# Routing in smaller batches, norms with the sign turned, a shared layer by channels, and weight copies ahead of row copies

## The chip, the cores and the metric

The kernel runs on one core of a Trainium2 chip. Its engines are TensorE (PE, with its weight loads listed as PEld), VectorE (DVE), ScalarE (ACT), GpSimd (POOL) and SyncE (SP), which here only issues DMAs. Each engine works through its own list of instructions in order, and semaphores tie the lists together. The metric is device time in microseconds of one launch, lower is better; times are medians of several runs.

## The reference, cut to what matters

The input `x` is 16 x 256 tokens of 128 channels, so 4096 tokens. One block of a recurrent mixer (RWKV) is followed by a layer norm and a mixture of experts with a shared expert:

```python
x = _layernorm(x + _L0_attn_ref(x, ...))     # three norms inside, k/v/r, a scan over time, channel mixing
# _L0_ffn_ref
ys = _geglu(xf @ Ws1 + bs1) @ Ws2 + bs2      # shared expert, 256 hidden channels
logits = (xf @ Wr + br) / TAU                # 12 experts, the two best per token
top_val, top_idx = jax.lax.top_k(logits, 2)
top_w = jax.nn.softmax(top_val, axis=-1)
act = _geglu(einsum('nd,edh->enh', xf, We1) + be1)   # 384 hidden channels for each expert
yE = einsum('enh,ehd->end', act, We2) + be2
x = _layernorm(x + ys + einsum('end,ne->nd', yE, w))
```

All in float32. The kernel computes an expert only for the tokens that chose it.

## The kernel before

**First stages.** The 4096 tokens are cut into 8 chunks of 512 (`CH`, `CT = 4` tiles of 128 each). Every chunk passes norm 0, norm 1, keys, values and receptance, the scan, the output projection, norm 2, the channel mixing, norm 3, the turn into channels (`xnT_all`), the router and the shared expert. These steps are small functions (`stats1(c)`, `turn2(c)`, `hidden(c, j)` and so on), and each engine has a list of calls, written out by hand, that sets its order: chunks overlap like the stages of a pipeline. A norm is `stats` on DVE, `deviation(c, n)` on POOL (`over_deviation`, L811 to L819: add epsilon, negate the mean, raise to the power -1/2, multiply) and `apply` on ACT.

**Routing.** `chosen(v, b)` picks the two best experts of a batch of chunks on DVE, `prefix(b)` counts on PE, `placed(v, b)` turns the counts into places, and `scatter_rows` on POOL sends the rows with 64 indirect DMAs (two per tile of tokens) into `dispatched_rows`, a region for each expert. `BATCH` gives the chunks of a batch: four batches of two chunks. When the last batch is placed, `find_tiles` on DVE writes `pad_at` and signals `rows_known`; SP then sends 12 blocks of padding, and `tell_tiles` writes `word`, the list of tiles with their experts, and signals `tiles_known`.

**Shared expert.** `shared_gate`, `shared_up`, `shared_gelu`, `shared_act`; `shared_back` multiplies by `Ws2` with tokens as output rows (eight 128-wide matmuls and four with the bias), `shared_take` on ACT copies the result into `xnT_all`, and POOL adds it to `x_all` (L1129, eight adds of 128x512 at the head of the expert stage, `sh_added`).

**Loop over tiles.** There are 75 tiles (`TILES`) of 128 dispatched rows. SP copies the rows of tile n into `xg[n % 10]` (`load_rows`, L1093, 68 KB) and the expert's first weights into `w1[n % 5]` (`load_weights`, L1100, 384 KB). PE does, for tile n: `gate_of` and `up_of` (three products each, L1244), `turn_x(n + 2)` (L1236), `second(n - 1)` (L1262, and the bias L1231). ACT does `gelu_of`; DVE does `act_of(n)` (L1165) and `give_y(n - 1)` (L1172); POOL sends each result to `routed_rows`. Once in five tiles DVE also does `where_to` (L1150 to L1157), which computes for the next five tiles where their rows go, and for that waits until all five have been copied:

```python
for n in range(r * U, (r + 1) * U):
    v.wait_ge(x_loaded2[n % XB], (n // XB + 1) * 16)
```

It stands in DVE's list after `act_of(n)` and `give_y(n - 1)` for n = 2, 7, 12, ..., 67 (`if n % U == 2 and n + U < TILES: where_to(n // U + 1)`), so 14 times in the loop, and `where_to(k + 1)`, at n = 5k + 2, needs rows 5k + 5 to 5k + 9. Two waits of the loop matter beside it: `up_of(n)` waits for `act_of(n - 1)`, whose bank it overwrites, and `load_weights(n)` waits for `up_ready` of tile n - 5, whose weight buffer it overwrites. SP's list reads rows five tiles ahead of weights: after five row copies, `load_weights(n)`, `load_rows(n + 5)` for each n.

**End.** SP waits for all results, loads the two results of each token (`y_first` into `x0_all`, `y_second` into `xnT_all`), PE adds three terms in PSUM for each chunk (`add_to`, L1290), and the last norm follows on DVE, POOL and ACT.

## Time and profile before

| what | value |
| --- | --- |
| median of 3 runs | 470.45 us (469.33 to 470.94) |
| profiled execution, its own time | 469.14 us |
| span of its trace | 467.4 us |
| busy PE / DVE / ACT / POOL | 405.8 / 313.4 / 273.0 / 271.0 us |
| mean granted PE clock | 0.961 of full |

The trace has three parts: the first stages with routing up to about 252 us, the loop over tiles from 261.67 us to about 436 us, and the end. In the trace L1093 is a copy of rows, L1100 a copy of weights, L1150 the first instruction of a `where_to`. The span starts with the first instruction, and the 1.7 us between span and time lie around it. A time that a row gives for PE ends where the model of the pipelined matmul puts it.

### The profile page before, as it was taken

How to read it: one execution, taken by the hardware profiler on the slowest of the kernel's cores; microseconds unless marked ns; L12 is line 12 of the kernel's file. 1: busy time of each engine (PE TensorE's matmuls, PEld its weight loads, DVE VectorE, ACT ScalarE, POOL GpSimd, SP SyncE). 2: the span in 40 equal slices, each digit the busy share in tenths (PEclk: the TensorE clock that was granted, in tenths of full speed). 3: DMA queues.
4: the chain of work that ended last, by engine and by line, in shares of the span. 5: the costliest groups of instructions: out<-in, count | busy, mean ns of one | idle time of the engine just before them, and what ended most of it. 6: DMA issues, size and time to landing. Idle time of an engine off the chain costs nothing.

```text
span 467.4 us, 9975 instructions
## 1 busy us (share of the span) xinstructions
PE 405.8 (87%) x2658; PEld 321.1 (69%) x2658; DVE 313.4 (67%) x1057; ACT 273.0 (58%) x648; POOL 271.0 (58%) x360
## 2 busy tenths in 40 slices
PE   0176799998989897999998698999999999999991
PEld 0133466765655583877666698999999999999530
DVE  4669889999999999644831555555655555655162
ACT  2476599998978766595532354455545555554055
POOL 4766757586567867788777543444444444444264
PEclk9997789999999898999999599999999999999997
DMA  5389900000001000111132566666666666764393
GB/s 153 90 169 356 280 1 0 1 1 2 0 2 42 24 31 14 44 37 48 61 108 67 181 225 222 233 232 241 243 233 239 228 230 231 249 234 174 120 325 113
DMA packets 49261, 64.09 MB, mean 137 GB/s; under 512 B 9916, under 2 KB 32188, under 8 KB 49208
## 3 DMA queue, kind: packets, MB, share of 16 engines
q1 hardware_dynamic: 44760, 54.08, 34.8%
q0 software_dynamic: 4448, 9.38, 6.0%
q8 instruction: 24, 0.39, 0.4%
q14 instruction: 29, 0.24, 0.2%
HBM read 20.87 MB, written 13.91 MB: 74 GB/s over the span
## 4 chain that ended last, share of the span: by engine, by line
PE 54%; DVE 12%; POOL 12%; issue 9%; DMA 5%; ACT 4%; SPq 2%; ACTq 0%; DVEq 0%; POOLq 0%
PE bank L1244 23%; PE bank L1262 11%; POOL dispatched_rows L407 7%; PE bank L956 4%; PE bank L974 4%; PE bank L907 2%; PE bank L908 2%; DVE bst L478 2%; PE bank L1236 2%; PE bank L985 1%; DMA xnT_all<-routed_rows 1%; PE bank L986 1%; POOL rstd L817 1%; POOL frs L817 1%; ACT z L683 1%
## 5 line engine op out<-in xcount | busy, mean ns | idle before, releaser
L1133 POOL DMA_INDIRECT routed_rows<-yo,goes_to x75 | 71.8, 958 | 102.3 <-DVE yo L1172 99.6
L1244 PE MATMUL bank<-xT,w 128*128 128x128 f32 x900 | 119.6, 284 | 5.8 <-DMA w<-we_sb 3.9
L1244 PEld LDWEIGHTS bank<-xT,w 128*128 128x128 f32 x900 | 108.9, 195 | 8.3 <-issue 5.8
L1208 ACT ACTIVATE gl<-bank,tile_bias 128x128 f32<-128x128 f32 x225 | 66.7, 365 | 60.3 <-PE bank L1244 59.3
L1165 DVE SCALAR_TENSOR_TENSOR actT<-bank,tile_bias,gl 128x128 f32<-128x128 f32 x225 | 65.7, 345 | 31.4 <-PE bank L1244 25.4
L407 POOL DMA_INDIRECT dispatched_rows<-rows_all,slot_i x64 | 64.2, 1003 | 18.5 <-issue 17.3
L1262 PE MATMUL bank<-we_sb,actT 128*128 x450 | 62.7, 276 | 1.0 <-DVE yo L1172 0.9
L1262 PEld LDWEIGHTS bank<-we_sb,actT 128*128 128x128 f32 x450 | 56.1, 192 | 1.4 <-issue 1.4
L1172 DVE TENSOR_SCALAR yo<-bank,goes 128x128 f32<-128x128 f32 x75 | 26.3, 350 | 33.6 <-PE bank L1231 33.4
L956 PE MATMUL bank<-xk,wfk_sb 128*128 128x512 f32 x64 | 34.2, 649 | 5.2 <-DVE xk L575 4.2
L1202 ACT ACTIVATE xT<-bank 128x128 f32<-128x128 f32 x75 | 20.8, 277 | 28.9 <-PE bank L1236 28.2
L817 POOL TENSOR_TENSOR rstd<-veps,half 128x4 f32<-128x4 f32 x32 | 35.0, 1093 | 2.5
L907 PE MATMUL bank<-hT,mixa 128*128 128x512 f32 x48 | 28.4, 677 | 4.4 <-ACT hT L711 4.1
L974 PEld LDWEIGHTS bank<-wfv_sb,kf 128*128 128x128 f32 x256 | 29.5, 192 | 2.8 <-ACT kf L768 2.2
L893 PE MATMUL bank<-ident,z 128*128 128x128 f32 x64 | 10.7, 294 | 23.5 <-ACT z L683 23.5
L974 PE MATMUL bank<-wfv_sb,kf 128*128 128x128 f32 x256 | 30.2, 276 | 0.5 <-ACT kf L768 0.5
L814 POOL TENSOR_TENSOR veps<-mv,eps 128x4 f32<-128x4 f32 x32 | 8.7, 272 | 34.2 <-DVE mv L483 31.1
L893 PEld LDWEIGHTS bank<-ident,z 128*128 128x128 f32 x64 | 8.0, 151 | 28.5 <-issue 22.8
L558 DVE RECIPROCAL rec<-nd 128x512 f32<-128x512 f32 x8 | 26.7, 3341 | 0.7 <-POOL nd L861 0.7
L908 PE MATMUL bank<-hT,mixb 128*128 128x512 f32 x48 | 26.6, 638 | 0.0
L612 DVE SCALAR_TENSOR_TENSOR below_m<-bank,v_sb,below_p 128x512 f32<-128x512 f32 x16 | 11.9, 747 | 18.8 <-PE bank L1009 10.4
L956 PEld LDWEIGHTS bank<-xk,wfk_sb 128*128 128x128 f32 x64 | 11.6, 201 | 15.8 <-issue 7.0
(204 smaller groups left out, 824.2 us busy)
## 6 DMA issues: line engine op xcount, KB each, us to landing
w<-we_sb SPq DMA_DIRECT2D x75, 384.0 KB, 2.7
x_all<-dispatched_rows SPq DMA_DIRECT2D x75, 68.0 KB, 2.0
we_sb<-we SPq DMA_DIRECT2D x1, 4608.0 KB
rows_all<-x SPq DMA_DIRECT2D x8, 256.0 KB, 2.7
x_all<-routed_rows SPq DMA_DIRECT2D x8, 256.0 KB, 4.8
xnT_all<-routed_rows SPq DMA_DIRECT2D x8, 256.0 KB, 6.6
out<-x_all SPq DMA_DIRECT2D x8, 256.0 KB, 2.3
routed_rows<-yo,goes_to POOLq DMA_INDIRECT x75
```

What stands on the lines that cost most here:

```text
L407: ng.indirect_dma_start(dispatch, bass.IndirectOffsetOnAxis(ap=slot_i[:, k, n:n + 1], axis=0), rows_all[:, n, :], None).then_inc(s["dispat ...
L558: nv.reciprocal(rec[:, :], nd[:, 1, :]).then_inc(s["rec_ready"], 1)
L817: ng.tensor_tensor(rs[:, :], ve[:, :], half[:, :], ALU.pow).then_inc(step, 1)
L907: nt.matmul(o, mixa[:, n, :], hT[:, :, 1:T + 1], start=True, stop=False)
L908: nt.matmul(o, mixb[:, n, :], hT[:, :, 0:T], start=False, stop=True).then_inc(s[name], 1)
L956: nt.matmul(pf[j % 2][:, :], wfk_sb[:, j * P:(j + 1) * P], xk2[:, :], start=True, stop=True).then_inc(s["fk_ready"], 1)
L974: last = nt.matmul(pkv[:, n * P:(n + 1) * P], kf[:, j, n * P:(n + 1) * P], wfv_sb[:, j, :], start=j == 0, stop=j == HF - 1)
L1133: ng.indirect_dma_start(routed, bass.IndirectOffsetOnAxis(ap=goes_to[n // U % DB][:, n % U:n % U + 1], axis=0), yo[n % YO][:, :], None).th ...
L1165: nv.scalar_tensor_tensor(actT[n % UA][:, at], ps_a[j][:, 0:P], tile_bias[:, j, n:n + 1], gl[n % 2][:, at], ALU.add, ALU.mult).then_inc(s2 ...
L1208: na.activation(gl[n % 2][:, j * P:(j + 1) * P], ps_g[j][:, 0:P], ACT.Gelu, bias=tile_bias[:, HK + j, n:n + 1]).then_inc(s2["gelu_ready"], 1)
L1244: return nt.matmul(to[:, 0:P], w1[m][:, off:off + P], xT[m][:, :], start=True, stop=True)
L1262: nt.matmul(ps_y[:, 0:C], actT[m][:, j * P:(j + 1) * P], we2_sb[:, ds(e, 1), j, :].rearrange("p a c -> p (a c)"), start=j == 0, stop=False)
```

## The change

1. `BATCH` has six batches: chunk 0, chunks 1 and 2, chunks 3 and 4, then 5, 6 and 7 alone. The lists of DVE, ACT, POOL and PE for the first stages are written in another order, with the 64 scatters spread otherwise over POOL's list: 26 stand behind the last `deviation(7, "3")`, 28 before.
2. In norms 0, 1 and 2 the mean is no longer negated. `mv` has a third column of -1, one POOL instruction multiplies mean and -1 by the deviation, and ACT so applies the norm with its sign turned; the weights `ln0w`, `LN1W`, `LN2W` are negated once in `prepare` (`turned_sign`).
3. `shared_back` gives channels as output rows with two 128x512 matmuls, and `shared_take` on DVE adds the bias and the chunk of `xnT_all` in place. The eight adds on POOL are gone. In the end `add_turned` (four 128-wide matmuls a chunk) takes `xnT_all` back to tokens, and `y_second` lands in `x_all`, whose rows are 136 numbers apart.
4. SP issues the five weight copies of tiles 0 to 4 as soon as `tiles_known` is there, ahead of the wait for the scatters. Behind them stand the five row copies, and then, for n = 5 and up, `load_rows(n)` and `load_weights(n)`.

```diff
-    BATCH = ((0, 2), (2, 4), (4, 6), (6, 8))
+    BATCH = ((0, 1), (1, 3), (3, 5), (5, 6), (6, 7), (7, 8))
...
-        y_second = xnT_all[:, :].rearrange("p (n c) -> p n c", c=C)
+        y_second = x_all
...
+            def shared_take(c):
+                if c == 0:
+                    v.wait_ge(s["bias_loaded"], 2 * 16)
+                v.wait_ge(s2["sh_out"], c + 1)
+                at = slice(c * W, (c + 1) * W)
+                nv.scalar_tensor_tensor(xnT_all[:, at], sh_y[:, :], bs2_col, xnT_all[:, at], ALU.add, ALU.add).then_inc(s2["sh_taken"], 1)
...
-            shared_act(2, 0); shared_act(2, 1); logits(7); chosen(v, 3); shared_act(3, 0); shared_act(3, 1)
-            placed(v, 3, pT[:, PT_PREFIX]); find_tiles(); shared_act(4, 0); shared_act(4, 1); tell_tiles()
+            shared_act(3, 1); shared_take(2); placed(v, 5, pT[:, PT_PREFIX]); shared_act(4, 0); shared_act(4, 1)
+            shared_take(3); find_tiles(); shared_act(5, 0); shared_act(5, 1); shared_take(4); tell_tiles()
...
-                over_deviation(g, veps[n], negm[n], rstd[n], nmr[n], mv[n], s["pow" + n], c, s["nmr" + n])
+                if n == "3":
+                    over_deviation(g, veps[n], negm3, rstd[n], nmr3, mv[n], s["pow" + n], c, s["nmr" + n])
+                else:
+                    ng.tensor_tensor(veps[n][:, :], mv[n][:, :, 1], eps4[:, :], ALU.add).then_inc(s["pow" + n], 1)
+                    g.wait_ge(s["pow" + n], c * 2 + 1)
+                    ng.tensor_tensor(rstd[n][:, :], veps[n][:, :], half[:, :], ALU.pow).then_inc(s["pow" + n], 1)
+                    g.wait_ge(s["pow" + n], c * 2 + 2)
+                    ng.tensor_tensor(both[n][:, :, :], mv[n][:, :, 0:3:2], over(rstd[n][:, :], 2), ALU.mult).then_inc(s["nmr" + n], 1)
...
-                for n in range(CT):
-                    for j in range(HS):
-                        nt.matmul(sh_y[:, n * P:(n + 1) * P], ash[:, j, n * P:(n + 1) * P], ws2_sb[:, j, :],
-                                  start=j == 0, stop=False)
-                    last = biased(sh_y[:, n * P:(n + 1) * P], BS2, C)
+                for j in range(HS):
+                    last = nt.matmul(sh_y[:, :], ws2_sb[:, j, :], ash[:, j, :], start=j == 0, stop=j == HS - 1)
...
-            sp.wait_ge(s2["tiles_known"], 1)
-            sp.wait_ge(s["dispatched"], SLOTS // P * 16)
-            sp.wait_ge(s2["pads_placed"], E * 16)
...
+            sp.wait_ge(s2["tiles_known"], 1)
+            for n in range(U):
+                load_weights(n)
+            sp.wait_ge(s["dispatched"], SLOTS // P * 16)
+            sp.wait_ge(s2["pads_placed"], E * 16)
             for n in range(U):
                 load_rows(n)
-            for n in range(TILES):
+            for n in range(U, TILES):
+                load_rows(n)
                 load_weights(n)
-                if n + U < TILES:
-                    load_rows(n + U)
...
-            g.wait_ge(s["dispatched"], SLOTS // P * 16)
-            for c in range(CH):
-                at = slice(c * CT, (c + 1) * CT)
-                g.wait_ge(s2["sh_taken"], c + 1)
-                ng.tensor_tensor(x_all[:, at, :], x_all[:, at, :], shared_out[:, at, :], ALU.add).then_inc(s2["sh_added"], 1)
...
+            def add_turned(c):
+                for n in range(CT):
+                    at = slice(n * P, (n + 1) * P)
+                    nt.matmul(banks[c][:, at], xnT_all[:, c * W + n * P:c * W + (n + 1) * P], ident[:, :], start=n == 0, stop=False)
```

**SP's list where the expert stage begins.** `w1_0` to `w1_4` are the weight buffers; `x0_all` stands for the row buffers `xg`, which lie in it. The last block of padding and what follows it, before:

```order
L1082 DMA dispatched_rows<-pad_rows 16x1088
L1088 TENSOR_LOAD word [waits e_pads_placed,dispatched,e_tiles_known]
L1093 ISA
L1093 DMA x0_all<-dispatched_rows 128x136
L1088 TENSOR_LOAD word
```

The same place now, and further down where the row copies begin:

```order
L1098 DMA dispatched_rows<-pad_rows 16x1088
L1108 TENSOR_LOAD word [waits e_tiles_known]
L1112 REGISTER_ALU
L1112 ISA
L1112 DMA w1_0<-we1_sb 128x768
```

```order
L1112 DMA w1_4<-we1_sb 128x768
L1100 TENSOR_LOAD word [waits e_pads_placed,dispatched]
L1105 ISA
L1105 DMA x0_all<-dispatched_rows 128x136
L1100 TENSOR_LOAD word
```

The first weight copy stood behind five row copies; now all five weight copies stand between the padding and the first row copy, and the wait for the scatters comes after them.

**SP's list at rows 9.** Before, from the weight copy of tile 4 to that of tile 5 (the row copy between them is that of tile 9):

```order
L1100 DMA w1_4<-we1_sb 128x768
L1088 TENSOR_LOAD word
L1093 ISA
L1093 DMA x0_all<-dispatched_rows 128x136
L1096 TENSOR_LOAD word
L1100 REGISTER_ALU [waits e_up_ready]
L1100 ISA
L1100 DMA w1_0<-we1_sb 128x768
```

Now, from the row copy of tile 8 on; the weight copy is that of tile 8 and the row copy behind it that of tile 9:

```order
L1100 TENSOR_LOAD word
L1105 ISA
L1105 DMA x0_all<-dispatched_rows 128x136
L1108 TENSOR_LOAD word
L1112 REGISTER_ALU [waits e_up_ready]
L1112 ISA
L1112 DMA w1_3<-we1_sb 128x768
L1100 TENSOR_LOAD word
L1105 ISA
L1105 DMA x0_all<-dispatched_rows 128x136
L1108 TENSOR_LOAD word
```

Row copy 9 stood ahead of the first weight copy that waits for `up_ready`; now it stands behind four of them, the last of which waits for tile 3. The same holds for every later tile: row copy n stood behind the wait for tile n - 10, and stands behind the wait for tile n - 6.

**DVE's list where the last batch is placed.** The first row is the last instruction of the last `placed`, `pad_at` opens `find_tiles`. Before:

```order
L377 CAST slot_i<-slot 128x2x8 [waits route]
L617 CAST pad_at<-run 1x12
L619 TENSOR_SCALAR run_i<-run 128x12 [waits e_tiles_step]
L620 MEMSET wait_here 1x1 [waits e_tiles_step]
L621 TENSOR_SCALAR run_t<-run_i 128x12
```

Now:

```order
L378 CAST slot_i<-slot 128x2x4 [waits route]
L619 SCALAR_TENSOR_TENSOR below_m<-bank0,v_sb,below_p 128x512 [waits e_sh_out,e_sh_gelu,e_sh_up]
L619 SCALAR_TENSOR_TENSOR below_m<-bank2,v_sb,below_p 128x512 [waits e_sh_gelu,e_sh_up]
L627 SCALAR_TENSOR_TENSOR xnT_all<-bank7,braw,xnT_all 128x512 [waits e_sh_out]
L631 CAST pad_at<-run 1x12
L633 TENSOR_SCALAR run_i<-run 128x12 [waits e_tiles_step]
L634 MEMSET wait_here 1x1 [waits e_tiles_step]
```

Three instructions of the shared expert of chunks 4 and 3 have moved ahead of `find_tiles`, and with it of `rows_known`, for which SP waits.

## Rows read from the trace of the kernel before

**Rows 1.** The page: the chain that ended last, by line.

```profile
PE bank L1244 23%; PE bank L1262 11%; POOL dispatched_rows L407 7%; PE bank L956 4%; PE bank L974 4%; PE bank L907 2%; PE bank L908 2%; DVE bst L478 2%; PE bank L1236 2%; PE bank L985 1%; DMA xnT_all<-routed_rows 1%; PE bank L986 1%; POOL r
```

**Rows 2.** Timeline, the loop: start us, us, engine, line, operation, [idle before <-releaser].

```profile
314.30 0.51 SPq L1100 DMA_DIRECT2D w<-we_sb  x1
...
314.55 1.56 PE L1244 MATMUL bank<-xT,w 128*128 128x128 f32 x12
...
315.42 0.34 SPq L1093 DMA_DIRECT2D x_all<-dispatched_rows  x1
...
316.77 1.56 PE L1244 MATMUL bank<-xT,w 128*128 128x128 f32 x12
...
317.36 0.17 DVE L1150 TENSOR_TENSOR other<-x_all,own_code 128x5 f32<-128x5 f32 x1
```

**Rows 3.** Timeline, DVE alone, near the end of the loop.

```profile
419.60 0.17 DVE L1150 TENSOR_TENSOR other<-x_all,own_code 128x5 f32<-128x5 f32 x1 [0.48 <-DMA x_all<-dispatched_rows]
```

**Rows 4.** Timeline, the one place where the loop waited for rows.

```profile
283.45 0.89 PE L1244 MATMUL bank<-xT,w 128*128 128x128 f32 x6
...
284.62 0.17 DVE L1150 TENSOR_TENSOR other<-x_all,own_code 128x5 f32<-128x5 f32 x1 [2.78 <-DMA x_all<-dispatched_rows]
...
285.35 0.87 DVE L1165 SCALAR_TENSOR_TENSOR actT<-bank,tile_bias,gl 128x128 f32<-128x128 f32 x3
...
285.75 1.01 PE L1244 MATMUL bank<-xT,w 128*128 128x128 f32 x6 [1.42 <-DVE actT L1165]
...
287.79 1.58 PE L1244 MATMUL bank<-xT,w 128*128 128x128 f32 x12
```

**Rows 5.** One line (L1100): duration ns min/median/max, first to last start.

```profile
L1100 SPq FUSED_REGOPS  x75: 46/52/57, 258.6 to 423.2; - x75
L1100 SPq DMA_DIRECT2D w<-we_sb x75: 486/492/595, 258.7 to 423.3; - x75
```

**Rows 6.** Timeline, PE alone: the two restarts after a wait.

```profile
34.17 1.64 PE L907 MATMUL bank<-hT,mixa 128*128 128x512 f32 x2 [3.26 <-ACT hT L711]
...
180.65 2.20 PE L956 MATMUL bank<-xk,wfk_sb 128*128 128x512 f32 x3 [2.25 <-DVE xk L575]
```

**Rows 7.** Stretches: us, busy of PE, PEld, DVE, ACT, POOL; PEclk, DMA, GB/s.

```profile
34.83:38.24 3.41, 3.41 (x9) 1.59 (x8) 3.38 (x7) 2.36 (x7) 2.37 (x3) 0.53 0.79 225
80.00:100.00 20.00, 19.86 (x108) 13.45 (x107) 19.76 (x55) 17.59 (x36) 13.91 (x21) 1.00 0.01 1
181.60:185.02 3.42, 3.42 (x5) 1.24 (x4) 3.35 (x7) 1.65 (x4) 2.77 (x4) 0.53 0.00 0
284.00:287.41 3.41, 1.94 (x14) 1.52 (x14) 2.52 (x11) 1.08 (x4) 0.66 (x1) 1.00 0.59 206
...
46.00:48.00 2.00, 2.00 (x10) 2.00 (x11) 1.92 (x17) 1.53 (x3) 1.54 (x3) 0.50 1.02 401
50.00:52.00 2.00, 2.00 (x4) 0.74 (x3) 1.73 (x10) 1.73 (x5) 0.40 (x1) 0.57 1.06 293
```

**Rows 8.** Timeline, from the last scatters to the first tiles.

```profile
229.69 0.15 DVE L617 CAST pad_at<-run 1x12 int32<-1x12 f32 x1
...
231.26 15.06 SPq L1082 DMA_DIRECT2D dispatched_rows<-pad_rows  x12
...
254.02 1.56 PE L1043 MATMUL bank<-of_expert,be_sb 12*128 12x75 f32 x12
254.42 3.78 SPq L1093 DMA_DIRECT2D x_all<-dispatched_rows  x5
...
259.81 0.27 DVE L1150 TENSOR_TENSOR other<-x_all,own_code 128x5 f32<-128x5 f32 x1 [8.21 <-DMA x_all<-dispatched_rows]
...
260.12 1.19 DVE L1152 TENSOR_TENSOR moved<-x_all,other 128x10 f32<-128x10 f32 x1
...
261.67 2.90 PE L1244 MATMUL bank<-xT,w 128*128 128x128 f32 x12 [3.90 <-DMA w<-we_sb]
```

**Rows 9.** One line (L407), the scatters: duration ns, first to last start.

```profile
L407 POOL DMA_INDIRECT dispatched_rows<-rows_all,slot_i x64: 954/958/1433, 142.0 to 251.6; - x64
```

More of the change, by code:

```diff
@@ new lines, in attention_vector @@
+            weigh_v(5); output(4); stats1(7); states(5); stats2(4); maximum(6); logits(2); gaps(6); carried(5)
+            x3(3); stats3(3); mix(4); one_over(5); output(5); chosen(v, 1); weigh_v(6); stats2(5); states(6)
+            carried(6); placed(v, 1, pT[:, PT_PREFIX]); maximum(7); gaps(7); mix(5); x3(4); logits(3)
+            one_over(6); output(6); stats3(4); weigh_v(7); stats2(6); states(7); carried(7); x3(5); stats3(5)
+            mix(6); one_over(7); logits(4); output(7); chosen(v, 2); shared_act(0, 0); stats2(7)
@@ L987, in rwkv @@
                 last.then_inc(s["po_ready"], 1)
-            def biased(to, row, width):
-                return nt.matmul(to, ones_bf[:, :], bias_rows[:, ds(row, width)], start=False, stop=True)
             def bank_read(c, j, of, first, other):
@@ L1296, in experts_tensor @@
             for c in range(CH - 1):
-                add_to(c, x_all, first=True)
+                add_turned(c)
             t.wait_ge(s2["yo_ready"], TILES)
-            add_to(CH - 1, x_all, first=True)
+            add_turned(CH - 1)
             for c in range(CH):
```

211 lines of the change are left out of this document (107 added, 104 removed).

## The prediction

> **What bounds the kernel now.** I read the chain of waits first, by line [rows 1]. Its largest shares are L1244 and L1262, the matmuls of the loop over tiles, then the scatters L407. So two places count: the loop, bound by PE, and the handover to it, where PE waits. The loop's timeline comes next [rows 2]. Tile 22 begins on PE at 314.55 and tile 23 at 316.77, so a tile takes 2.22 us and PE has no gap. Look there at two other rows: SP issues the rows of tile 29 at 315.42, and the `where_to` that waits for them (L1150) starts at 317.36, hardly before DVE must go on to tile 23. Row copies arrive just in time even now. Third, the one place where they did not [rows 4]: L1150 waited 2.78 us until 284.62, and PE then stood still for 1.42 us. At the handover [rows 8] SP sends padding for 15.06 us from 231.26, row copies from 254.42, and PE's first tile waits for its weights until 261.67. The first stages keep both PE and DVE over 98% busy between 80 and 100 us [rows 7], so a new order alone has little to give there.
>
> **Row copies behind the weights' waits: the large term.** In the new list the rows of tile 5k+9 stand behind the weight copy of tile 5k+8, and that waits for `up` of tile 5k+3. But `where_to(k+1)` stands in DVE's list ahead of `act_of(5k+3)` and needs these rows, and PE's `up(5k+4)` waits for `act_of(5k+3)`. So each of the 14 `where_to` becomes a closed chain, priced step by step:
> - end of `up(5k+3)` to SP's weight copy: 0.1 us from the register step to the DMA [rows 5], with the semaphore and one more step 0.3 (an estimate);
> - weight copy to row copy on SP: 314.30 to 315.42, 1.12 us [rows 2];
> - row copy to the start of L1150, whose data it is: 315.42 to 317.36, 1.94 us [rows 2];
> - L1150 to PE's next matmul: 284.62 to 285.75, 1.13 us [rows 4].
>
> That is 4.49 us. Without a wait, `up` of one tile ends at 316.11 (314.55 + 1.56), and that of the next begins 0.67 us after 316.77 (twelve matmul instructions take 1.56, six take 0.89 [rows 2, 4]), at 317.44: 1.33 us. PE thus gains a hole of 4.49 - 1.33 = 3.16 us. Behind the wait at 285.75 the next tile began 2.04 us later [rows 4] where 1.55 is normal, so add 0.49. Five tiles take 5 x 2.22 + 3.65 = 14.8 us at full clock.
>
> **The clock on top.** PE's restart after 3.26 us idle at 34.17 and after 2.25 us at 180.65 [rows 6] was each followed by a stretch at 0.53 granted clock, from 34.83 and from 181.60 [rows 7], that is nearly all at 1.2 GHz instead of 2.4. Half the speed for 3.4 us costs 1.7 us. After the shorter hole of 1.42 us the clock stayed at 1.00, from 284.00 on [rows 4, 7]. A hole of 3.16 lies with the first two. I take 1.2 us for each of the 14: most of 1.7, less for a slow stretch that begins inside the hole, and for DVE's 0.49, which it covers. Bounds are 0 and 1.7. Five tiles then take 16.0 us (14.8 to 16.5), against 11.25 now (284.62 to 419.60 in twelve steps [rows 3, 4]).
>
> **The handover.** The early weight copies look like a gain: PE waited 3.90 us for weights at 261.67 [rows 8]. But they stand on SP behind the padding, and `find_tiles`, which starts the padding, moves behind two `shared_act` and one `shared_take`. I put `pad_at` at 235 instead of 229.69. Then padding runs from 236.6 to 251.7, five weight copies at about 1.05 us (0.49 issue [rows 5] and the load of `word`) to 256.9, and the first row copy goes out at 257.5, not 254.42. The first `where_to` starts at 262.9 instead of 259.81 (3.1 later), but its steps take some 0.2 us each as in the loop, not 1.19 [rows 8], since the POOL adds that ran beside them are gone. DVE's first `act_of` so starts at 263.6, within 0.2 of now. Nothing is gained. If `find_tiles` came at its old time, 3 us would be, and this end stays in the range. From 263.6, tiles 1 to 3, the first of them at half clock as now, bring `up(3)` to its end at 270.1 and the second `where_to` to 273.5.
>
> **The scatters.** POOL's 64 scatters end at 251.6 [rows 9] and bind SP now. Two fewer behind the last norm would free about 2.5 us (1.26 us each), but SP is not ready for them until 256.9. So batches of other sizes and 26 instead of 28 weigh nothing, unless POOL ends more than 5 us later than now. The two further batches repeat `chosen` and `placed` on DVE, after the stages in which DVE is full. For the new order of the first stages, the shorter norm chain on POOL and the cheaper second layer together I take -1 us, from bounds of -6 and +4. The second layer and `tell_biases` (254.02 now [rows 8]) lie hidden in front of the first tile; if that cover were gone, each microsecond would count once.
>
> **The end.** `y_second` now lands in rows of 512 bytes. Both kinds of transfer stand in the loading of the experts' weights: 401 GB/s with pieces of 3 KB (46 to 48 us) and 293 GB/s with pieces of 512 bytes (50 to 52 us) [rows 7]. For 2.1 MB that is 5.2 against 7.2 us. Part of it hides behind the final norm, so +1 us (0 to 2). The Trainium skill, DMA: Bandwidth & Descriptors, section Specifications, says that pieces from 512 bytes up reach line rate, which would make this term 0; the rows here say otherwise.
>
> **The sum.** The second `where_to` at 273.5, the third at 289.5, the last, twelve steps of 16.0 later, at 481.5, against 419.60: +61.9. Behind the last one PE resumes within its hole and slow stretch, +0.9. With -1 and +1 that is +62.8 on the profiled execution's 469.14, so 532; I take 531. The runs' median is 1.3 us above the profile, which the range covers.
>
> **The rivals.**
> 1. *The clock stays.* The hole comes as above, but no slow stretch: 14 x 1.2 = 17 less, 514 us. For it speaks the hole of 1.42; against it those of 2.25 and 3.26. The Trainium skill, TensorE: Matmul & The Clock Gate, section HAM oscillation — how this bites in real kernels, warns only of idle gaps longer than this hole. By that rule it would be this case; the restart at 180.65 contradicts it, since a hole of 2.25 was enough. Chance 0.27.
> 2. *The handover pays and the loop does not lose.* Place: row copy against DVE, once in five tiles. It decides whether rows are there 0.2 us (1.33 - 1.13) after `up(5k+3)` ends; I get 3.36. For it speaks that SP today meets its weight waits late, with the awaited tile long done, so a wait in its list costs nothing now. Against it, that this holds only while SP lags, and that here the awaited tile is the one before the hole. The wait of rows 4 would go too (-2.1), with -1 and +1: 467 us. Chance 0.04.
> 3. *Row copies land later.* They now go out just behind 384 KB of weights and beside POOL's scatters; one microsecond more on each of the 14 gives 545 or above. Against it: the copy at 315.42 went out behind weights as well. Chance 0.07.
> 4. *The order has no effect,* all is hidden: within 0.3% of now. Chance 0.02.
>
> **How the numbers follow.** My case, holes with a slower clock after most, has 0.60: 531 us, its own range 522 to 540. The range 507 to 545 takes in rival 1 with 7 us below it for a handover and first stages that gain (3 + 5, less 1), and on top 7 us if every hole brings the full 1.7 (14 x 0.5) and 7 for slower copies. Outside are rivals 2 and 4 and most of 3. A measurement of this kernel can tell about 0.3% from no change. Slower by more: 0.95; faster: 0.04, rival 2; same: 0.01.
>
> **What would show it.** In the trace of the changed kernel L1150's counterpart should wait for `x_all<-dispatched_rows` some 3 to 5 us, 14 times, with PE idle 3 us each time behind DVE's `actT`; the distance of two `where_to` should be 16 us; SP's weight copy should start 0.3 us after `up` ends; the granted clock in the loop should fall from 1.00 to about 0.9, where rival 1 has it at 1.00. The first row copy should go out near 257.5, right behind five weight copies. I am wrong if distances stay at 11.25, which would mean that SP runs further ahead than its list allows; or, in size, if landing or clock differ from the rows used.

## The result, and where the time went

The changed kernel takes 551.0 us (median; 550.6 to 554.2) against 470.1 us before: 1.172 of the time, 95% interval 1.167 to 1.178. In a later group, which also held the kernel before, it took 546.2 us (1.159, 1.155 to 1.163). The forecast was 531, its range ended at 545. Direction and mechanism are those of the forecast, the size is not. The profiled execution of the changed kernel took 554.23 us, its span is 552.5.

The chain of waits, by line, has turned over [rows 1]. SP's queue and DMA, which had 2% and 5% of it, now hold a quarter:

```profile
PE 37%; DVE 23%; SPq 18%; issue 9%; DMA 8%; POOL 4%; ACT 1%; DVEq 0%; ACTq 0%; POOLq 0%
PE bank L1253 14%; DMA x_all<-dispatched_rows 6%; SPq L1112 5%; PE bank L1271 5%; SPq L1108 3%; SPq L1105 3%; PE bank L981 3%; SPq L1100 3%; PE bank L999 2%; DVE rec L565 2%; DVE bst L485 2%; PE bank L932 2%; PE bank L933 2%; SPq L1098 1%;
```

Who waits for whom in the loop (284 to 520 us), in total, times, longest. VectorE's L1159 is the first instruction of `where_to`; before, eight of these 14 waited for rows, 5.7 us in sum and 2.78 at most [rows 3, 4]:

```profile
DVE other L1159 <- DMA x_all<-dispatched_rows: 65.4, 14, 5.6
...
PE bank L1253 <- DVE actT L1174: 46.7, 14, 4.3
```

One of the 14 closed chains, on the timeline of the changed kernel (start, duration, engine, line):

```profile
396.28 1.56 PE L1253 MATMUL bank<-xT,w 128*128 128x128 f32 x12
...
398.25 0.49 SPq L1112 DMA_DIRECT2D w<-we_sb  x1
...
398.51 0.89 PE L1253 MATMUL bank<-xT,w 128*128 128x128 f32 x6
...
399.33 0.34 SPq L1105 DMA_DIRECT2D x_all<-dispatched_rows  x1
401.26 0.17 DVE L1159 TENSOR_TENSOR other<-x_all,own_code 128x5 f32<-128x5 f32 x1 [4.32 <-DMA x_all<-dispatched_rows]
...
402.38 1.00 PE L1253 MATMUL bank<-xT,w 128*128 128x128 f32 x6 [2.99 <-DVE actT L1174]
...
403.55 1.64 PE L1271 MATMUL bank<-we_sb,actT 128*128 x6
...
405.09 2.36 PE L1253 MATMUL bank<-xT,w 128*128 128x128 f32 x12
```

Read it from the top: `up` of tile 5k+3 ends at 397.84 (396.28 + 1.56), SP's weight copy starts 0.41 later, the row copy 1.08 behind it, `where_to` 1.93 behind that, and PE resumes 1.12 later: 4.54 us where the forecast had 4.49. PE does `gate` of the next tile in between and stands still for 2.99 us. Soon behind it, the six instructions of L1271 take 1.64 us (0.83 at 397.78, ahead of the pause), and the tile after it 2.36 us for twelve instead of 1.56. The clock of the same place (stretch, busy time of PE, PEld, DVE, ACT, POOL; granted clock, DMA share, GB/s):

```profile
400.00:402.00 2.00, 0.00 (x0) 0.00 (x0) 0.64 (x5) 0.00 (x0) 0.00 (x0) 1.00 0.34 113
402.00:404.00 2.00, 1.58 (x9) 1.33 (x10) 1.88 (x8) 0.28 (x1) 0.62 (x1) 0.84 0.00 0
404.00:406.00 2.00, 2.00 (x11) 1.94 (x11) 0.35 (x1) 0.13 (x1) 0.34 (x1) 0.50 0.66 226
```

So the slow stretch, at 1.2 instead of 2.4 GHz, begins here some 1 us after PE is back at work. Whole distances between two `where_to`, same columns:

```profile
302.11:319.77 17.66, 13.34 (x100) 12.81 (x100) 6.52 (x24) 6.03 (x20) 4.79 (x5) 0.90 0.44 151
...
386.41:401.26 14.85, 11.80 (x100) 11.25 (x100) 6.53 (x25) 5.81 (x20) 4.79 (x5) 1.00 0.52 180
401.26:417.50 16.24, 13.28 (x100) 12.73 (x100) 6.52 (x24) 6.03 (x20) 4.79 (x5) 0.89 0.47 164
...
433.79:450.94 17.15, 14.25 (x100) 13.95 (x100) 6.99 (x25) 6.03 (x20) 4.79 (x5) 0.80 0.45 156
```

The second row is the chain alone at full clock: 14.85, forecast 14.8. The third holds the slow stretch above, which ends at 406.8, and takes 16.24. The fourth takes 17.15: its slow stretch is twice as long and unbroken. It began in the pause, ahead of PE's return at 434.92, and went on to about 440.9 (same columns):

```profile
433.50:434.50 1.00, 0.00 (x0) 0.00 (x0) 0.60 (x4) 0.00 (x0) 0.00 (x0) 0.79 0.02 8
...
439.50:440.50 1.00, 1.00 (x7) 1.00 (x6) 0.41 (x2) 0.40 (x2) 0.39 (x1) 0.50 0.12 39
440.50:441.50 1.00, 1.00 (x9) 1.00 (x9) 0.65 (x2) 0.28 (x1) 0.00 (x0) 0.80 0.18 61
```

The first row has the shorter stretch and a row copy that landed late.

The handover, on the timeline [rows 8]:

```profile
244.04 0.15 DVE L631 CAST pad_at<-run 1x12 int32<-1x12 f32 x1
...
245.60 15.07 SPq L1098 DMA_DIRECT2D dispatched_rows<-pad_rows  x12
...
261.23 5.19 SPq L1112 DMA_DIRECT2D w<-we_sb  x5
...
267.09 4.92 SPq L1105 DMA_DIRECT2D x_all<-dispatched_rows  x6
...
270.99 2.85 PE L1253 MATMUL bank<-xT,w 128*128 128x128 f32 x12 [0.28 <-issue]
```

Padding and weight copies lie 0.56 us apart, weight and row copies 0.67, so SP has no idle time there, as forecast, but `pad_at` comes at 244.04 instead of 235.

### The profile page after: what moved, and what is told of

Same layout as the page of the kernel before. It is cut to its first block, busy times and chain, and to the rows that moved or that the text cites. A ratio compares the mean times of both kernels' runs of the same rounds, so it can differ in the third digit from the quotient of the medians.

```text
span 552.5 us, 9846 instructions
## 1 busy us (share of the span) xinstructions
PE 436.3 (79%) x2580; PEld 342.6 (62%) x2580; DVE 332.9 (60%) x1119; ACT 277.3 (50%) x646; POOL 256.5 (46%) x328
## 3 DMA queue, kind: packets, MB, share of 16 engines
q1 hardware_dynamic: 47400, 54.08, 29.5%
## 4 chain that ended last, share of the span: by engine, by line
PE 37%; DVE 23%; SPq 18%; issue 9%; DMA 8%; POOL 4%; ACT 1%; DVEq 0%; ACTq 0%; POOLq 0%
PE bank L1253 14%; DMA x_all<-dispatched_rows 6%; SPq L1112 5%; PE bank L1271 5%; SPq L1108 3%; SPq L1105 3%; PE bank L981 3%; SPq L1100 3%; PE bank L999 2%; DVE rec L565 2%; DVE bst L485 2%; PE bank L932 2%; PE bank L933 2%; SPq L1098 1%; POOL frs L833 1%
## 5 line engine op out<-in xcount | busy, mean ns | idle before, releaser
L1253 PE MATMUL bank<-xT,w 128*128 128x128 f32 x900 | 140.7, 311 | 47.0 <-DVE actT L1174 46.7
L1253 PEld LDWEIGHTS bank<-xT,w 128*128 128x128 f32 x900 | 126.8, 219 | 51.5 <-DVE actT L1174 49.4
L1217 ACT ACTIVATE gl<-bank,tile_bias 128x128 f32<-128x128 f32 x225 | 69.2, 366 | 69.3 <-PE bank L1253 67.7
L1174 DVE SCALAR_TENSOR_TENSOR actT<-bank,tile_bias,gl 128x128 f32<-128x128 f32 x225 | 67.7, 346 | 35.7 <-PE bank L1253 31.0
L1271 PE MATMUL bank<-we_sb,actT 128*128 x450 | 70.9, 299 | 1.3 <-DVE yo L1181 0.9
L1271 PEld LDWEIGHTS bank<-we_sb,actT 128*128 128x128 f32 x450 | 63.6, 213 | 3.3 <-issue 3.2
L1159 DVE TENSOR_TENSOR other<-x_all,own_code 128x5 f32<-128x5 f32 x15 | 2.5, 166 | 76.3 <-DMA x_all<-dispatched_rows 76.3
L999 PEld LDWEIGHTS bank<-wfv_sb,kf 128*128 128x128 f32 x256 | 29.4, 192 | 2.3 <-ACT kf L789 1.9
L861 POOL TENSOR_TENSOR rstd<-veps,half 128x4 f32<-128x4 f32 x24 | 27.2, 1132 | 1.9
L1245 PE MATMUL bank<-ident,x_all 128*128 128x128 f32 x75 | 22.6, 302 | 6.8 <-DMA x_all<-dispatched_rows 6.8
L785 ACT ACTIVATE kf<-bank 128x512 f32<-128x512 f32 x32 | 18.8, 591 | 12.3 <-PE bank L981 12.2
```

The costliest lines, as they stand in the source:

```text
L999: last = nt.matmul(pkv[:, n * P:(n + 1) * P], kf[:, j, n * P:(n + 1) * P], wfv_sb[:, j, :], start=j == 0, stop=j == HF - 1)
L1174: nv.scalar_tensor_tensor(actT[n % UA][:, at], ps_a[j][:, 0:P], tile_bias[:, j, n:n + 1], gl[n % 2][:, at], ALU.add, ALU.mult).then_inc(s2 ...
L1217: na.activation(gl[n % 2][:, j * P:(j + 1) * P], ps_g[j][:, 0:P], ACT.Gelu, bias=tile_bias[:, HK + j, n:n + 1]).then_inc(s2["gelu_ready"], 1)
L1253: return nt.matmul(to[:, 0:P], w1[m][:, off:off + P], xT[m][:, :], start=True, stop=True)
L1271: nt.matmul(ps_y[:, 0:C], actT[m][:, j * P:(j + 1) * P], we2_sb[:, ds(e, 1), j, :].rearrange("p a c -> p (a c)"), start=j == 0, stop=False)
```

## The experiments

Sixteen kernels (two of them twice) ran in five groups, each beside the kernel before, and ratios are to that. Every group had another chip. In three groups the kernel before took 470 to 471 us, in the first and the fourth 497 and 495. On those two chips VectorE and ScalarE stand still for up to 17 us at a time, mostly between 200 and 275 us (the waits of those traces name "remote"; the other traces have none). SP's padding is longer there too: 29.2 to 29.7 us in the kernels with the old order of the first stages and 16.5 to 20.4 in those with the new one, where the other chips show 15.1 to 15.6. So the ratios of these two groups say little about the handover. Distances in the loop are as elsewhere (16.58 us there with closed chains, 16.54 and 16.77 on other chips).

**1. The loop: which part of the change makes the chain.** Rows five tiles ahead again in the changed kernel, early weights kept:

```diff
-            for n in range(U, TILES):
-                load_rows(n)
-                load_weights(n)
+            for n in range(TILES):
+                if n >= U:
+                    load_weights(n)
+                if n + U < TILES:
+                    load_rows(n + U)
```

> The changed kernel with one edit on SP: the five weight copies stay early, but behind the first five row copies the list is again row copy n+5 behind weight copy n, so that rows run five tiles ahead. My theory (all of the loop's loss is the closed chain row copy - weight wait - where_to): the distance of two where_to falls from 16.8 to 11.25 us, the granted clock in the loop is 1.00 again, and what is left against the kernel before is the later handover (second where_to at 284 against 273) and 0 to 1 us at the end: 480 to 483 us. Rival (the early weights, the shared layer or the changed buffers slow the loop as well): distances stay above 12 us and the time above 490 us.

Measured: 1.0069 (1.0036 to 1.0102). The whole time is less than expected (480 to 483 us would be 1.020 to 1.027). The likely reason, which no run shows, is that on this chip the old order loses in the padding, 29.4 us against 16.5, what the later `pad_at` costs the new one. For the loop my theory held: the mean distance of two `where_to` is 11.37 us, at full clock, and PE is busy for 147.11 of 147.84 us:

```profile
304.31:452.15 147.84, 147.11 (x1308) 144.83 (x1307) 86.80 (x313) 75.81 (x263) 62.24 (x65) 1.00 0.66 232
```

The new SP list of part 4, put alone into the kernel before:

> The kernel before with part 4 of the change alone (five weight copies ahead of the wait for the scatters, then rows and weights of the same tile in turn). My theory: distances of 16 to 17 us as in the changed kernel, 13 times 5.5 us or 72 us, the first hole on top and 1 to 2 us less at the handover: 540 to 546 us. Rival (the clock is pulled down by more than the holes, the first stages have a part in it): distances of 14.8 us at full clock and 515 us.

Measured: 1.1498 (1.1462 to 1.1535), 74 us, mean distance 16.58 us, as expected (540 to 546 us would be 1.148 to 1.160). The full-clock distance appears here too, beside one with a clock of 0.80:

```profile
407.68:424.63 16.95, 14.01 (x100) 13.71 (x100) 6.92 (x24) 6.03 (x20) 4.80 (x5) 0.80 0.45 158
424.63:439.74 15.11, 11.81 (x100) 11.25 (x100) 6.53 (x24) 5.81 (x20) 4.80 (x5) 1.00 0.50 176
```

So the row copies' place in SP's list is needed and is enough for what the loop loses; the first stages have no part in that. Third, SP's list stays as changed and VectorE's list moves:

```diff
-                if n % U == 2 and n + U < TILES:
+                if n % U == 4 and n + U < TILES:
```

> The changed kernel with SP's list as it is, and where_to two tiles later in VectorE's list (n = 4, 9, 14 ... instead of 2, 7, 12 ...). The rows of tile 5k+9 still go out only behind up(5k+3), but where_to no longer stands ahead of the act that PE needs next. My theory: copies land 3.4 us behind up(5k+3) and where_to comes up about 3.3 us behind it, so it waits 0 to 0.5 us, PE has no holes, distances are 11.25 us: 480 to 484 us, the same as with rows ahead. Rival (late row copies hurt by themselves, through turn_x or because SP then waits for where_to in turn): 490 us or more.

Measured: 1.0206 (1.0163 to 1.0249), 506 us on this slower chip; as a ratio that is my theory (480 to 484 us would be 1.020 to 1.029). Mean distance 11.77 us. This is one of the fourteen:

```profile
318.61 0.58 SPq L1105 DMA_DIRECT2D x_all<-dispatched_rows  x1
...
318.85 0.17 DVE L1159 TENSOR_TENSOR other<-x_all,own_code 128x5 f32<-128x5 f32 x1 [1.23 <-DMA x_all<-dispatched_rows]
...
319.22 1.77 PE L1253 MATMUL bank<-xT,w 128*128 128x128 f32 x12
```

VectorE still waits 1 to 1.5 us in eight of them (2.92 once), but PE's next step mostly does not stand behind it. It did once: behind the wait of 2.92 us PE paused for 1.63 us until 425.85, and the granted clock of that distance is 0.86. Two tiles of distance in one list give back 13 times 4.8 us against `b_new_list` on the same chip. Nothing was done to SP or the copies, so late row copies cost little by themselves.

**2. The clock.** Ten products that nobody uses, put into the hole:

```diff
                 gate_of(w, n, r)
+                if w == U - 1 and n + 1 < TILES:
+                    t.wait_ge(s2["xT_ready"], n + 2)
+                    for _ in range(10):
+                        nt.matmul(ps_x[:, P:2 * P], ident[:, :], ident[:, :], start=True, stop=True)
                 up_of(w, n)
```

> The changed kernel with ten 128x128 products of the identity that nobody uses, into free columns of ps_x, between gate and up of the last tile of every five (n = 4, 9, ... 69), so right in the hole that PE has there: ten products take about 2.7 us, the hole is 2.9 to 4.4. It does more work and computes the same. My theory (part of the loss is the slower clock after the hole, 1.4 us for one slow stretch, 2.3 us for two): PE is never idle, the granted clock stays near 1.00, and the distance of two where_to falls from 16.5 to about 14.9 us: 521 to 527 us, a ratio of 1.11 against 1.159. Rival (the slow stretches come from something else than PE's pause, the products only add to the chain): 546 us or more, a ratio of 1.16.

Measured: 1.1478 (1.1448 to 1.1507), 540.4 us: faster, but less gained than I expected (1.11). The 1.159 is from another group and chip, and this kernel's trace has the slow stretch of point 5, which the trace behind 1.159 has not. The traces show the loop by itself: from the second to the last `where_to` it takes 205.0 us, against 218.0 and 215.1 in the changed kernel's two. The trace has one hole filled like this (L1292 are the extra products), and the clock of the distance that ends in it:

```profile
409.63 2.40 PE L1292 MATMUL bank<-ident 128*128 128x128 f32 x20
412.60 0.17 DVE L1159 TENSOR_TENSOR other<-x_all,own_code 128x5 f32<-128x5 f32 x1 [5.26 <-DMA x_all<-dispatched_rows]
```

```profile
396.82:412.60 15.78, 14.04 (x120) 13.49 (x120) 6.52 (x24) 5.81 (x20) 4.78 (x5) 1.00 0.49 169
```

Eleven of the 13 distances now show a clock of 1.00; in the changed kernel it was one of 13 (two of 13 in its second trace). More work made the kernel faster, so the slow stretches do come from PE's pauses. The mean distance fell from 16.77 and 16.54 to 15.77, not to 14.9: VectorE's waits for rows grew (the 13 after the second `where_to` sum to 65.2 us, 60.2 in the changed kernel), so part of the gain went to later row copies. Why they land later there, no run tells.

**3. The early weight copies.** In the kernel before, alone:

> The kernel before with the five weight copies early and the row copies still five tiles ahead. My theory: PE's first tile no longer waits 3.9 us for weights but begins when its row copy has landed, near 258 us; VectorE's first act then hangs on where_to(0), so only part of it is gained: 468 to 469 us, 1 to 2 us less than before. Rival A (all 3.9 us are gained): 466 us. Rival B (weight copies beside the scatters delay the scatters, and with them the rows): 470 us or more.

Measured: 0.9989 (0.9965 to 1.0012): smaller than the interval. This is one of the slower chips: the padding lasts 29.35 us, to 278.2, and the weight copies follow at 278.80, so SP had next to no idle time to use, and the run does not test early copies where it has. In the changed kernel, taken back (all of SP's list as before, so that parts 1 to 3 are left):

> The changed kernel with all of SP's list as before (rows five tiles ahead, no early weight copies). My theory: in the changed kernel SP is never idle between find_tiles and the first rows (15.1 us of padding to 260.7, then 5.2 us of weights), so the early copies delay the rows by 5.2 us and save at most 3.9 us at the first tile; taking them back gains 1 to 3 us against the same kernel with them: a ratio of about 1.002 to 1.005 if that kernel has 1.007. Rival (early weights help, as they do in the kernel before by 0.75 us): 1 to 2 us slower than with them.

Measured: 1.0097 (1.0067 to 1.0127), 475.7 us, in one group with the changed kernel at 546.2. Its ratio does not compare with 1.0069, which is from a slower chip, so my 1 to 3 us were not tested by the time. The first tile can be compared. Without early copies:

```profile
265.67 2.90 PE L1252 MATMUL bank<-xT,w 128*128 128x128 f32 x12 [3.83 <-DMA w<-we_sb]
```

and with them, in the changed kernel's second trace, whose `pad_at` is 0.3 us earlier:

```profile
266.01 2.90 PE L1253 MATMUL bank<-xT,w 128*128 128x128 f32 x12 [0.29 <-issue]
```

The wait for weights is gone, and the rows come later by as much: from `pad_at` to the first tile it takes 26.25 us without early copies and 26.89 with them. "Nothing is gained" held.

**4. The first stages.** Here the forecast was furthest off. The yardstick of this group, the changed kernel again:

> The changed kernel as it is, beside the other runs of this group, as their yardstick: 1.172 of the kernel before, unless the chip counts for something; on the chip of the first group, by the kernel before with the new SP list alone (1.150), 1.15 to 1.18.

Measured: 1.159, 546.2 us. Part 3 (shared layer) alone, then part 2 (norms) alone:

> The kernel before with part 3 of the change alone (second layer of the shared expert by channels, shared_take on VectorE, no adds on POOL, y_second into x_all, add_turned at the end). My theory: about even. VectorE has three shared_take of 0.75 us ahead of find_tiles, 1.5 to 2 us later, the first where_to takes 1 us less without POOL's adds beside it, the load at the end costs 1 us: 0 to +2 us. Rival A (the end gains, since the eight POOL adds and the wait for them go): -2 us. Rival B (VectorE is the bound and shared_take counts in full, with the extra slow-down of what runs beside it): +4 us or more.

> The kernel before with part 2 of the change alone (mean no longer negated in norms 0 to 2, weights negated once). POOL saves 24 short instructions, VectorE gains three in prepare and ACT's first affine waits for them. My theory: POOL is not the bound, so -1 to 0 us; 469.5 to 471 us. Rival A (the norm chain is on VectorE's way, each norm 0.2 us shorter): -3 us. Rival B (the three negations, 1 to 2 us at the start where VectorE prepares weights, push everything back): +1 to +2 us.

Measured: 0.9996 (0.9974 to 1.0019) and 0.9943 (0.9922 to 0.9964). The norms gain 1.8 us by the medians and 2.7 by the ratio, more than my -1 to 0 and near rival A's -3; in the trace the last `x3` of the first stages starts at 211.65 instead of 212.62. Both parts together:

> The kernel before with parts 2 and 3 of the change (norms, shared second layer) and nothing else: order, four batches and SP's list as before. It splits the 4.6 us that parts 1 to 3 together cost. My theory: the two add up (0.9943 and 0.9996), 467 to 469 us, so that the new order with six batches alone costs 6 to 8 us. Rival (norms or shared layer only hurt together with each other, by what runs at the same time on POOL and VectorE): 471 us or more, and the order costs 4 us or less.

Measured: 0.9898 (0.987 to 0.9927), on the fourth group's slower chip. So they went side by side with parts 1 to 3 on a chip of 471 us:

> Parts 2 and 3 of the change alone once more, now side by side with parts 1 to 3 on one chip, since the two stood on different chips (0.9898 where the kernel before took 495 us, 1.0097 where it took 471 us). My theory: parts 2 and 3 gain 0.6 to 1.0% on any chip: a ratio of 0.990 to 0.994. Rival (their gain was that chip's, with its long pauses around the handover): 0.997 or more.

> Parts 1 to 3 with SP's list as before, on the same chip as parts 2 and 3 alone. My theory: part 1 (the written order with six batches, find_tiles behind three more instructions) costs 7 to 9 us: a ratio 0.015 to 0.02 above that of parts 2 and 3. Rival (half of the difference was the chips'): 0.010 or less above it.

Measured: 0.9952 (0.9931 to 0.9974), 468.0 us, and 1.013 (1.0078 to 1.0182), 478.4 us. Part 1, the written order with six batches, costs 10.4 us, the other two give back 3. The six times of the second kernel lie between 472.75 and 480.25, and its trace has the slow stretch of point 5; with the time of the earlier group (475.7), whose trace has not, part 1 would cost 7.7.

Are the batches the cause?

```diff
-    BATCH = ((0, 1), (1, 3), (3, 5), (5, 6), (6, 7), (7, 8))
+    BATCH = ((0, 1), (1, 3), (3, 5), (5, 7), (7, 8))
```

> The changed kernel with five batches instead of six: chunks 5 and 6 are routed together, where chunk 6 was; all other calls stand where they stood. My theory (VectorE is the bound of the first stages and a batch costs some 25 small instructions of 0.17 to 0.2 us, two table loads of 1.28 us on ACT lie in its way too): the last placed comes 2 to 3 us earlier, and with it padding, weights and rows: 543 to 544 us, ratio 1.153 to 1.156 against 1.159. Rival (a batch costs nothing, other work fills the time; the larger last batches come later): no change or 1 us slower.

Measured: 1.168 (1.1657 to 1.1702), above both theories, though 1.159 is from another chip. My theory fell: the last `slot_i` starts at 236.10, in the changed kernel's second trace at 236.12, with two table loads of 1.28 us on ACT fewer on the way. The edit also took one `chosen` out from ahead of the last `x3`, and that `x3` starts at 217.58 instead of 217.70; in the gap VectorE waits 2.77 us for ScalarE's `hT` at 203.40, which it did not in the changed kernel. So one batch less moved neither point. The loss of the order is older than the last two batches. Up to the last `x3` (before, and changed kernel, second trace) VectorE, the fourth column, is busy for 11.1 us more, and that `x3` comes 5.1 us later:

```profile
0.00:212.60 212.60, 170.07 (x873) 114.64 (x873) 178.90 (x548) 155.52 (x287) 146.02 (x211) 0.95 0.23 69
```

```profile
0.00:217.70 217.70, 167.80 (x857) 112.10 (x857) 190.00 (x569) 157.09 (x289) 144.23 (x190) 0.96 0.23 69
```

By the instructions' own durations, which sum to 11.9 us more, 4.6 are routing (a fourth `chosen` and smaller batches), 3.4 the scan and its neighbours, which take longer each, and the rest `prepare`, the shared expert and `x3`. That VectorE is the bound there is not shown by it: in both kernels the step ahead of the last `x3` waits for PE, 5.15 us before and 2.88 now. Which calls of the new order cost the 5.1 us no run separates.

And `find_tiles` comes 3.0 us behind the last `slot_i`; before, it was 0.1 us:

```profile
236.12 0.17 DVE L378 CAST slot_i<-slot 128x8 uint32<-128x8 f32 x1
239.12 0.15 DVE L631 CAST pad_at<-run 1x12 int32<-1x12 f32 x1
```

That place was tried in two kernels, one with rows ahead and early weights, one with all of SP's list as before:

```diff
-            shared_act(3, 1); shared_take(2); placed(v, 5, pT[:, PT_PREFIX]); shared_act(4, 0); shared_act(4, 1)
-            shared_take(3); find_tiles(); shared_act(5, 0); ...
+            shared_act(3, 1); shared_take(2); placed(v, 5, pT[:, PT_PREFIX]); find_tiles(); shared_act(4, 0)
+            shared_act(4, 1); shared_take(3); shared_act(5, 0); ...
```

> The changed kernel with rows five tiles ahead and early weights, and find_tiles directly behind the last placed, ahead of two shared_act and one shared_take. My theory: the padding, and with it weights and rows, starts 2.9 us earlier (241.1 instead of 244.0), since SP's list from find_tiles to the first rows has no idle time, so 3 us less than with find_tiles where it stands: ratio about 1.001 if that kernel has 1.007. Rival (the scatters or the shared layer, now 3 us later, end last): less than 1 us gained.

> Parts 1 to 3 of the change with SP's list as before (1.0097), and find_tiles directly behind the last placed. My theory: part of what the order costs is this place: padding 2.9 us earlier, rows 2.9 us earlier as long as the scatters (last at 253.8) do not bind: rows at 255.6 instead of 258.5, 2.5 to 3 us less, ratio 1.003 to 1.005. Rival (the scatters or the shared layer bind instead): less than 1 us less, ratio 1.008 to 1.010.

Measured: 1.0039 (1.0007 to 1.007), where I had expected 1.001, and, on the fourth group's slower chip, 1.0041 (1.001 to 1.0073), as expected. In the first one's trace `pad_at` starts 0.08 us behind the last `slot_i` (241.50 and 241.42), so the padding does start 2.9 us earlier. The first is 1.9 us below `a_old_sp` in the same group, though its profiled execution had the slow stretch described next. No pair that differs in this place alone ran on one chip, so its worth in time, 1.4 and 2.6 us by the ratios across chips, is likely and not shown.

**5. Five microseconds that come and go.** The changed kernel's two traces part at 161 us. In both PE has paused for 3.09 us, in the recorded one and in the second:

```profile
162.07 1.09 PE L918 MATMUL bank<-ident,z 128*128 128x128 f32 x4 [3.09 <-DVE slot_i L378]
```

```profile
161.28 0.63 PE L918 MATMUL bank<-ident,z 128*128 128x128 f32 x4 [3.08 <-DVE slot_i L378]
```

The clock behind it, again first the recorded one:

```profile
163.00:164.00 1.00, 1.00 (x3) 0.48 (x3) 0.89 (x3) 0.80 (x2) 0.70 (x2) 0.50 0.19 65
165.00:166.00 1.00, 1.00 (x2) 0.34 (x1) 1.00 (x2) 1.00 (x2) 1.00 (x1) 0.50 0.21 70
```

```profile
163.00:164.00 1.00, 1.00 (x7) 0.54 (x5) 1.00 (x3) 0.53 (x2) 0.74 (x1) 1.00 0.20 70
165.00:166.00 1.00, 1.00 (x11) 1.00 (x10) 0.96 (x4) 0.97 (x2) 0.69 (x2) 1.00 0.25 73
```

The last `one_over` starts at 190.06 in the one and at 185.13 in the other, and the 4.9 us stay up to `pad_at` (244.04 and 239.12). The pause ends with `placed` of the second batch, which the new order puts into VectorE's full stretch; before, no pause of more than 1.35 us stands there. Ten traces have this order: five with a clock of 1.00 from 162 to 168 us, whose last `one_over` starts at 185.0 to 185.6; four with 0.50, at 190.1 to 190.8; and one with 0.58, at 188.5. So one more pause near 3 us can cost 5 us or nothing. A shorter one can be enough: at this place the kernel before has a pause of 1.35 us until 159.79, and `b_shared` one of 1.34 us until 160.89, and the clock behind them is, in this order:

```profile
161.00:164.00 3.00, 3.00 (x5) 1.02 (x4) 3.00 (x1) 2.80 (x7) 2.66 (x6) 0.50 0.07 23
```

```profile
161.00:164.00 3.00, 3.00 (x8) 1.33 (x9) 2.96 (x10) 2.89 (x5) 2.52 (x6) 1.00 0.14 46
```

**6. A faster kernel.** Parts 2 and 3, early weight copies, rows five tiles ahead, `where_to` one tile later, order and batches as before:

> A try at a better kernel: the kernel before with the norms and the shared second layer of the change, the five weight copies early, rows five tiles ahead, and where_to one tile later in VectorE's list (n = 3, 8, ...), with the order and the four batches of before. My theory: the early weights gain 1 to 2 us, the later where_to takes away the pause of 1.4 us that before has at 285.75, the rest is even: 466 to 469 us, ratio 0.991 to 0.997. Rival (early weights lose to the scatters, as in no gain): 470 to 472 us.

Measured: 0.9837 (0.9812 to 0.9862), 462.6 us, the shortest time of all and better than I expected. Here SP sends the weights while POOL still scatters, and PE starts 4.2 us earlier than before [rows 8]; 2.8 of them are parts 2 and 3 (258.91 in the trace of `b_parts_2_3_again`):

```profile
245.78 5.66 SPq L1110 DMA_DIRECT2D w<-we_sb  x5
...
253.73 8.03 SPq L1103 DMA_DIRECT2D x_all<-dispatched_rows  x10
...
257.50 2.90 PE L1253 MATMUL bank<-xT,w 128*128 128x128 f32 x12 [0.34 <-ACT xT L1211]
```

No `where_to` of its loop waits, the mean distance is 11.23 us. Which of its edits does it:

> The faster kernel (0.9837) with where_to back at n = 2, 7, 12 ...: parts 2 and 3, early weight copies, rows five tiles ahead. My theory: VectorE then waits again for rows now and then, the last where_to comes 1 to 2 us later than in that kernel; 464 to 465 us, ratio 0.986 to 0.989. Rival (where_to one tile later brought nothing, all of the gain is the early copies and the parts): the same 0.984.

> The faster kernel (0.9837) with SP's list as before, so without early weight copies; where_to at n = 3, 8 ... and parts 2 and 3 stay. My theory: PE's first tile waits 3.8 us for its weights again, of which 3 to 4 us are lost (first tile at 260.5 to 261.5 instead of 257.5): 465.5 to 467 us, ratio 0.990 to 0.993. Rival (VectorE's first act, not the weights, was the bound at the first tile): 463.5 us or less, ratio 0.986.

Measured, both on the fourth group's slower chip: 0.9819 (0.9767 to 0.9872) with `where_to` back, 0.9878 (0.9837 to 0.9918) without early copies, and 0.9898 for parts 2 and 3 with neither. Counted from the last, the later `where_to` brings 0.2%, which the intervals don't tell from nothing, and the early copies 0.8%, with intervals that just meet. The traces do not bear out the second: with early copies the way from `pad_at` to the first tile is 41.5 us, without them (parts 2 and 3) 40.2, and `pad_at` itself, which the edit does not touch, came 4.0 us earlier (237.91 and 241.89). The padding of 29 us leaves SP 2.2 us up to the first row copy in `b_parts_2_3`, on the chip of 471 us it is 7.7.

On chips of 470 and 471 us two traces can be set side by side, `b_best` and `b_parts_2_3_again`. That way takes 29.5 us in the one and 32.2 in the other, so the early copies gain some 2.6 us where SP would be idle; one execution of each, on two chips. From the second to the last `where_to` it is 146.0 us against 150.5; either the later `where_to` or the ten row copies that go out in one run can be the cause, and no run on such a chip separates them.

## Why the forecast was right in kind and short in size

The sum gave 531.9 us on the profiled execution, which took 554.23. The 22.3 us between them, by the forecast's own steps:

- **`pad_at`, 9.0 us.** Put at 235, it came at 244.04. 4.9 of it is the slow stretch behind the pause that ends at 162 us; without it the changed kernel has 239.12. That part is bad luck, but not the whole miss: without the stretch the kernel took 546.2 us, still above 545. The other 4.1 is the order: the last `x3` comes 5.1 us later and the way from there to the last `slot_i` takes 18.4 us instead of 17.0, where I had allowed for some 2 us beside `find_tiles`. The step that failed is the sentence that the further batches come "after the stages in which DVE is full": the first two are routed from 95 to 162 us, right in them, and PE's pause of 3.09 us ends with `slot_i` of the second. That much the traces show; which calls bring the 4.1 they do not. "A new order alone has little to give there" was right; I did not ask what it can take, though I had the row that shows no slack [rows 7].
- **First stages, 1.0 us.** The -1 did not come: parts 2 and 3 give 3 us, part 1 takes 8 to 10. About half of what it puts on `pad_at` hides in SP's idle time behind the padding: `a_old_sp` has `pad_at` 9.7 us later than before and its first tile 4.0 us later.
- **From `pad_at` to the second `where_to`, 1.6 us** (40.1 against 38.5). First row copy 267.09 against 257.5 and first `where_to` 273.22 against 262.9: both late by `pad_at` and less than 1.5 us more.
- **The loop, 10.0 us.** The second to the last `where_to` took 217.97 us, forecast 13 x 16.0. The chain at full clock was right (14.85 against 14.8). Row copies landed late mainly in the first periods: the 13 waits exceed 4.3 us by 4.3 us in sum. What remains, 217.97 - 13 x 14.85 - 4.3 = 20.6, is the clock: 1.6 us for each instead of 1.2. I had taken a slow stretch of one length, 1.7 us at most, and 1.2 for one that begins inside the hole. The eight distances at 0.89 or 0.90 have it, at 16.24 - 14.85 = 1.4; four (0.80 to 0.82) have one twice as long, at 17.15 - 14.85 = 2.3, and one has none. The mis-sized term is this one, and its reason was the wrong way round: stretches that begin inside the hole are the long ones.
- **Behind the last `where_to`, 0.7 us.** The end itself is as forecast: from the first load of results to the last instruction 28.1 us before and 28.5 in the changed kernel's second trace, 0.4 for the term of 1. The rates behind that term were not what they were said to be: the transfer of 50 to 52 us has packets of 2,048 bytes in the trace, not 512. Packets of 512 bytes come with the changed kernel's `y_second`.

Of the rivals, the first (clock stays, 514 us) is excluded by the clock rows and by `a_filled`. The row that spoke for it, a hole of 1.42 us without a slow stretch, had its counterpart in the same trace, the 1.35 us of point 5 with one. The Trainium skill, TensorE: Matmul & The Clock Gate, section HAM oscillation — how this bites in real kernels, warns only of longer gaps; the traces disagree with it, since gaps of 2.9 to 3.1 us were mostly enough. The second (handover pays, loop free) needed the rows within 0.2 us after `up` ends; they were there after 3.42 (401.26 - 397.84). The third (row copies land later) was given 0.07 and was in part true: 4.3 us of the miss, besides my own case and not instead of it. What should have been wider is the range: the clock came near its bound (1.6 of 1.7) and passed it after the long stretches, and `pad_at`, 9.0 us late, went past the +4 allowed for the first stages.

What was to be seen was seen: L1159 waits 4.2 to 5.6 us, 14 times; PE stops 2.9 to 4.3 us; SP's weight copy mostly 0.3 to 0.6 us behind the end of `up`; granted clock 0.88 from the second to the last `where_to`.

## What to carry to other kernels

When a copy moves behind a wait in a queue, follow the wait round: if the awaited engine needs the copy's data within its next step, the slack becomes a closed chain, paid each time; distance in either list breaks it (the consumer two tiles later did nearly as well as the copy five tiles earlier). Price a pause of TensorE near 3 us as the pause plus a slow stretch of either length (1.4 or 2.3 us here), and take both ends into the range; a pause of 1.35 us is not safe from it either. Before putting extra steps into an engine's list, look whether that engine has slack there; a cheap step in a full stretch costs itself and can make a pause elsewhere.

## What the runs showed of the hardware

- The clock behind a pause is not settled by its length. In the four traces with closed chains (the changed kernel twice, `b_new_list`, `a_five_batches`), of 52 distances 7 show 1.00, 34 show 0.89 or 0.90, and 11 show 0.80 to 0.84. In the 34 the slow stretch begins 0.2 to 1.8 us after PE resumes, in the 11 it begins 0.8 to 2.1 us before that and lasts twice as long. A pause of 3.09 us in two executions of one kernel was followed by 0.50 in one and 1.00 in the other, and so were pauses of 1.35 and 1.34 us at one place of two kernels.
- Useless matmuls in a hole gave back the clock: 11 of 13 distances at 1.00 instead of 1 or 2 of 13, and 10 to 13 us of the loop, although PE had more to do.
- A chip can be 5% slower with the same program (495 to 497 against 470 to 471 us), on two chips of five in these groups. There VectorE and ScalarE stand still between 200 and 275 us in waits of up to 17 us that the trace puts down to "remote", and SP's padding takes up to 29.7 us instead of 15.1. What holds them no run shows.
- With `y_second` landing in rows that lie 544 bytes apart, in packets of 512 bytes, the loads of the end ran at 319 to 354 GB/s, 337 in the mean (522 to 530 us, changed kernel's second trace); before, with rows that follow each other and packets of 2,048 bytes, at 339 to 404, 363 in the mean (442 to 450 us). The Trainium skill, DMA: Bandwidth & Descriptors, section Specifications, would have the two alike; the means lie 7% apart, in two kernels that differ in more than this, and the end is 0.4 us longer.
